# A two-layer Perceiver on one core: the two 1024 x 1024 layers of the last feed-forward as seven quadrant products, and another order of the cross-attention step

## The reference

```python
x = x + L0_xattn(layernorm(x), ctx)      # 16 heads, causal mask
x = x + L0_attn(layernorm(x))            # offsets, gate
x = x + L0_ffn(layernorm(x))             # quantised, 256-768-256
x = x + L1_xattn(layernorm(x), ctx)      # softmax over all 257 keys, no mask
x = x + L1_attn(layernorm(x))            # bias from Pluecker lines
x = x + L1_ffn(layernorm(x))
# L1_ffn, weights ternary, a scale s per output feature:
h = silu((x @ w1.T) * s1) * ((x @ w2.T) * s2)      # 256 -> 1024
h = gelu((h @ h1.T) * s_h1)                        # 1024 -> 1024
h = gelu((h @ h2.T) * s_h2)                        # 1024 -> 1024
return (h @ w3.T) * s3                             # 1024 -> 256
```

## Time and profile before

| what | us |
|---|---|
| median of 3 runs (lowest, highest) | 1780.78 (1777.43, 1781.12) |
| profiled execution, its own time | 1774.97 |
| its span | 1773.2 |
| PE busy, share of the span | 1539.7, 87% |
| DVE, ACT, POOL busy | 823.6, 567.8, 489.8 |
| L765, the two square layers, PE busy, 1024 records | 440.6 |
| L1014, a gelu of 128 x 512 on ACT, mean of one | 0.688 |
| L1547, `c_shift` on POOL, mean of one | 1.042 |
| a 257 KB context's DMA, median from issue to landing (page, part 6) | 2.6 |
| mean granted clock of PE in the profiled execution | 0.965 of full speed |

### The profile page before, as it was taken

How to read it: one execution, slowest core, us unless ns; L and a number is a source line. 1 busy time by engine, 2 the same in 40 slices (tenths; PEclk the granted TensorE clock), 3 DMA queues, 4 the chain that set the end, 5 groups by cost and what they waited for, 6 DMA issues and landing times.

```text
span 1773.2 us, 30285 instructions
## 1 busy us (share of the span) xinstructions
PE 1539.7 (87%) x11788; PEld 978.6 (55%) x11788; DVE 823.6 (46%) x1636; ACT 567.8 (32%) x1409; POOL 489.8 (28%) x581
## 2 busy tenths in 40 slices
PE   4887777891899999999985777699999999999999
PEld 3766665440777777777763555444454454445445
DVE  3889998568645655555554777620011002001000
ACT  2444333577434445444540222220111111101110
POOL 2444332001024545454444888600000000000000
PEclk9999999996899999999996999999999999999999
DMA  7000000000012221111100000020000000000000
GB/s 260 20 9 2 1 0 1 1 0 24 14 48 84 65 83 42 36 42 36 41 13 1 1 1 0 17 103 0 0 12 0 0 0 12 0 0 12 0 0 12
DMA packets 18198, 43.99 MB, mean 25 GB/s; under 512 B 3040, under 2 KB 5600, under 8 KB 16992
## 3 DMA queue, kind: packets, MB, share of 16 engines
q1 hardware_dynamic: 18144, 43.24, 7.4%
HBM read 41.14 MB, written 2.10 MB: 24 GB/s over the span
## 4 chain that ended last, share of the span: by engine, by line
PE 70%; DVE 16%; issue 5%; POOL 4%; ACT 4%; DVEq 1%; DMA 0%; SPq 0%; POOLq 0%; ACTq 0%
PE ps L765 25%; PE ps L411 12%; PE ps L604 6%; PE ps L610 6%; PE ps L417 4%; PE ps L630 4%; PE ps L780 3%; PE ps L582 2%; PE ps L641 2%; POOL lrn L1595 1%; DVE amax L1231 1%; DVE R L1054 1%; DVE nmx L1101 1%; DVE R L1092 1%; DVE R L1169 1%
## 5 line engine op out<-in xcount | busy, mean ns | idle before, releaser
L765 PE MATMUL ps<-R 128*128 128x512 f32 x1024 | 440.6, 592 | 0.0
L765 PEld LDWEIGHTS ps<-R 128*128 128x128 f32 x1024 | 194.3, 190 | 243.5 <-issue 243.5
L411 PE MATMUL ps<-R 128*128 128x128 f32 (+1 forms) x1344 | 308.2, 389 | 7.8 <-DVE R L1227 3.5
L411 PEld LDWEIGHTS ps<-R 128*128 128x128 f32 x1344 | 192.0, 196 | 122.8 <-issue 114.3
L1465 DVE TENSOR_TENSOR R<-ps,w3s 128x256 f32<-128x256 f32 x16 | 6.8, 425 | 465.1 <-PE ps L780 465.1
L1555 POOL TENSOR_TENSOR R<-R,c_inv 128x1024 f32<-128x1024 f32 x64 | 122.4, 1912 | 243.7 <-DVE c_inv L1389 243.7
L963 ACT ACTIVATE R<-ps,c_nmx 128x257 f32<-128x257 f32 x256 | 118.3, 474 | 104.7 <-DVE c_nmx L1378 104.7
L1354 DVE COPY R<-ps 128x512 f32<-128x512 f32 x128 | 88.5, 692 | 128.5 <-PE ps L630 128.5
L610 PE MATMUL ps<-x_wv,R 128*128 128x256 f32 x512 | 132.1, 382 | 0.0
L604 PE MATMUL ps<-R,x_wk 128*128 128x256 f32 x512 | 125.3, 387 | 2.3 <-DVE R L1365 1.2
L604 PEld LDWEIGHTS ps<-R,x_wk 128*128 128x128 f32 x512 | 94.4, 192 | 21.5 <-issue 9.2
(11 more groups left out here) (178 smaller groups left out, 2297.6 us busy)
## 6 DMA issues: line engine op xcount, KB each, us to landing
R<-in_ctxT SPq DMA_DIRECT2D x64, 257.0 KB, 2.6
R<-in_f_h SPq DMA_DIRECT2D x4, 1024.0 KB, 5.1
R<-in_f_h SPq DMA_DIRECT2D x1, 4096.0 KB, 12.6
R<-in_f_w SPq DMA_DIRECT2D x3, 1024.0 KB, 5.4
R<-in_ctxk SPq DMA_DIRECT2D x16, 128.0 KB, 2.3
out<-x SPq DMA_DIRECT2D x4, 512.0 KB, 2.6
x<-in_x SPq DMA_DIRECT2D x1, 1792.0 KB, 8.3
R<-in_a_wqkv SPq DMA_DIRECT2D x1, 768.0 KB, 8.5
```

The costliest lines, as they stand in the source:

```text
L411: r = mm(dst, w[:, ki, fo * P:(fo + 1) * P], src[:, ki, :], start=(ki == 0), stop=(ki == KI - 1))
L765: r = mm(ps[:, ring[o % 4], :], w[:, k, o * P:(o + 1) * P], src[:, k, :], start=(k == 0), stop=(k == NF1 - 1))
```

## The change

1. **Square layers.** `g_block` is replaced by straight code. The activations `f_a`, `f_b` of a block of 512 tokens are held as quadrants: features in two halves of 512, tokens in two halves of 256 (`B11`, `B12`, `B21`, `B22`), with four sums of them (`T1` to `T4`; `T3` overwrites `B12`). The weights are four 512 x 512 quadrants, three of which are used as they are (`A11`, `A12`, `A22`), and four sums (`S1` to `S4`). A layer is four groups `f`; in each, seven products of 4 matmuls with 256 columns go to halves of four PSUM banks (groups take banks 0 to 3 and 4 to 7 in turn). `g_open` makes the product of `A11` and `B11`, `g_close` the other six. ACT copies the first product to SBUF; seven additions on DVE make the partial sums and the four quadrants of the result (`g_close` of DVE, all 128 x 256); ACT applies four gelus of 128 x 256. In the first square layer DVE then makes the four `T` sums of the next layer (`g_sums`), and in `g_first` those of the first one. `g_turn(b+1)` now stands behind the two `g_open` that begin the second layer, and `g_norm(b+1)` on DVE behind the group f = 0 of the first.
2. **Weights.** They no longer lie in SBUF. During the cross-attention SP loads the quadrants of one layer (4 x 1 MB), POOL makes the four sums in 8 additions of 128 x 1024, one per step in steps 8 to 15 and 28 to 35, and SP stores them to a DRAM tensor. At n = 44 SP loads `w1`, `w2`, `w3` and the weights of the first two groups. `load_weights(g)` brings 7 x 128 x 512 values (1.835 MB) in two DMAs, with rows of 2 KB, into a ring of three places, once group g-3 is done: 32 such loads.
3. **Block edges.** `g_first` takes all eight banks, and its first output waits for fewer additions of the block before; `w3` takes four banks.
4. **Cross-attention.** `c_outputs` and `c_extract` are those of sequence n-2 and stand right behind the scores and the maxima; `c_keys` comes ahead of the wait for `c_otc`, and both halves of the values stand together between the two transposes. POOL's loop is written out; the others stay loops.

PE in the cross-attention, the step u = 1, before: L620 scores, L417 projection, L604 keys, L630 transposes, L610 values, L641 outputs.

The diff, cut to SP's loads, the steps of PE and DVE and the sums of POOL:

```diff
+            def load_quadrants(m):
+                for k, q in enumerate((0, 1, 3, 2)):
+                    sp.dma_start(c_quad[k], A["f_hq"][m, q].rearrange("p f c -> p (f c)")).then_inc(quad_in, 16)
+            def store_sums(m):
+                sp.wait_ge(quad_sum, 8 * (m + 1))
+                for k, q in enumerate((4, 5, 2, 1)):
+                    sp.dma_start(sums[m, k].rearrange("p f c -> p (f c)"), c_quad[q]).then_inc(quad_out, 16)
+            def load_weights(g):
+                m, f, r = g // 4 % 2, g % 4, g % 3
+                after(sp, g_prod, product_no(g - 3, 3))
+                sp.dma_start(f_wr[r][:, 0:3, :], A["f_hq"][m, 0:3, :, f, :].rearrange("q p c -> p q c"))\
+                    .then_inc(g_wr[r], 16)
+                sp.dma_start(f_wr[r][:, 3:7, :], sums[m, :, :, f, :].rearrange("q p c -> p q c"))\
+                    .then_inc(g_wr[r], 16)
             for i in range(T - 1):
                 for u in range(SPT):
                     n = SPT * i + u
                     sp.wait_ge(v_ready, n + 1)
                     sp.dma_start(c_ctx[u], A["ctxT"][n + SPT]).then_inc(ctx_in[u], 16)
-                if i < len(later):
-                    sp.wait_ge(f0_x, 1 + T)
-                    sp.dma_start(later[i][0], later[i][1]).then_inc(in_w["ffn"], 16)
+                    if n == 3:
+                        sp.wait_ge(f0_x, 1 + T)
+                        load_quadrants(0)
+                    if n == 18:
+                        store_sums(0)
+                    if n == 22:
+                        sp.wait_ge(quad_out, 64)
+                        load_quadrants(1)
+                    if n == 38:
+                        store_sums(1)
+                    if n == 44:
+                        sp.wait_ge(quad_out, 128)
...
                 c_scores(u)
+                if not (first and u < 2):
+                    if u == 2 and not first:
+                        pe.wait_ge(c_x, i)
+                    if u == 3 and not last:
+                        pe.wait_ge(s["xnT_copied"], N1 + i + 2)
+                    c_outputs(n - 2, (u + 2) % SPT)
+                more = not (last and u >= 2)
+                behind = not (first and u == 0)
+                if more:
+                    pe.wait_ge(ctx_shifted, n + 3)
+                    pe.wait_ge(k_copied, n + 2)
+                    c_keys((u + 2) % SPT)
                 after(pe, c_otc, n - 1)
...
                     c_query(i + 1)
-                more = not (last and u >= 2)
-                behind = not (first and u == 0)
-                if more:
-                    pe.wait_ge(ctx_shifted, n + 3)
-                    pe.wait_ge(k_copied, n + 2)
-                    c_keys((u + 2) % SPT)
                 if behind:
                     pe.wait_ge(c_nrm, n)
                     c_turn_probs(n - 1, (u + 1) % 2, 0)
                 if more:
                     pe.wait_ge(v_copied, n + 2)
-                    c_values((u + 2) % SPT, 0)
+                    for c in range(2):
+                        c_values((u + 2) % SPT, c)
                 if behind:
                     c_turn_probs(n - 1, (u + 1) % 2, 1)
-                if more:
-                    c_values((u + 2) % SPT, 1)
-                if behind:
-                    if u == 1 and not first:
-                        pe.wait_ge(c_x, i)
-                    if u == 2 and not last:
-                        pe.wait_ge(s["xnT_copied"], N1 + i + 2)
-                    if u == 3 and not last:
-                        pe.wait_ge(n_q2, i + 2)
...
+                    project(ps[:, 2 * (o % 4), :], f_w1, f_xnT, o)
+                    project(ps[:, 2 * (o % 4) + 1, :], f_w2, f_xnT, o).then_inc(g_ab, 1)
+            def product(g, w, src, k, bk, half):
+                for ki in range(4):
+                    r = mm(ps[:, 4 * (g % 2) + bk, half * HALF:(half + 1) * HALF], f_wr[g % 3][:, w, ki * P:(ki + 1) * P],
+                           src[:, k, ki, :], start=(ki == 0), stop=(ki == 3))
+                return r
+            def g_open(b, h, f):
+                g = 8 * b + 4 * h + f
+                src = f_b if h else f_a
+                pe.wait_ge(g_wr[g % 3], 32 * (g // 3 + 1))
+                if h == 0:
+                    pe.wait_ge(g_h, NF1 * b + (5, 7, 7, 7)[f])
+                else:
+                    pe.wait_ge(g_c, quadrant_no(8 * b + 3, 11))
+                if h or f >= 2:
+                    pe.wait_ge(g_sum, sum_no(g - 2, 11))
+                product(g, A11, src, B11, 0, 0).then_inc(g_p1, 1)
+            def g_close(b, h, f):
+                g = 8 * b + 4 * h + f
+                src = f_b if h else f_a
+                done = 8 * b + 4 * h + 4
+                used = h or f >= 2
+                if h:
+                    pe.wait_ge(g_c, quadrant_no(8 * b + 3, 12))
+                if h and f == 1:
+                    pe.wait_ge(g_xTc, min(2 * b + 4, 2 * NB))
+                pe.wait_ge(g_T2, done)
+                if used:
+                    pe.wait_ge(g_sum, sum_no(g - 2, 21))
+                product(g, S2, src, T2, 1, 0).then_inc(g_prod, 1)
+                pe.wait_ge(g_T3, done)
+                if used:
+                    pe.wait_ge(g_sum, sum_no(g - 2, 12))
+                product(g, S3, src, T3, 2, 0).then_inc(g_prod, 1)
+                pe.wait_ge(g_T1, done)
+                if used:
+                    pe.wait_ge(g_u, partial_no(g - 2, 4))
+                product(g, S1, src, T1, 3, 0).then_inc(g_prod, 1)
+                pe.wait_ge(g_p1c, g + 1)
+                product(g, A12, src, B21, 0, 1).then_inc(g_prod, 1)
+                pe.wait_ge(g_T4, done)
+                pe.wait_ge(g_u, partial_no(g, 2))
+                product(g, A22, src, T4, 1, 1).then_inc(g_prod, 1)
+                pe.wait_ge(g_u, partial_no(g, 3))
...
+                if not (first and u < 2):
+                    c_extract(n - 2, (u + 2) % SPT)
                 if u == 1 and not first:
...
-                    c_extract(n - 1, (u + 3) % 4)
...
+            def g_close(b, h, f):
+                g = 8 * b + 4 * h + f
+                bk = [[ps[:, 4 * (g % 2) + i, k * HALF:(k + 1) * HALF] for k in range(2)] for i in range(4)]
+                p1, u2 = f_p1[:, g % 2, :], f_u2[:, g % 2, :]
+                dve.wait_ge(g_prod, product_no(g, 6))
+                dve.wait_ge(g_p1c, g + 1)
+                v.tensor_tensor(u2, bk[1][0], p1, ALU.add).then_inc(g_u, 1)
+                dve.wait_ge(g_prod, product_no(g, 7))
+                dve.wait_ge(g_u, partial_no(g, 2))
+                v.tensor_tensor(f_u3, bk[2][0], u2, ALU.add).then_inc(g_u, 1)
+                dve.wait_ge(g_prod, product_no(g, 5))
+                dve.wait_ge(g_u, partial_no(g, 3))
+                after(dve, g_c, quadrant_no(g - 1, 22))
+                v.tensor_tensor(f_c22, bk[3][0], f_u3, ALU.add).then_inc(g_sum, 1)
+                v.tensor_tensor(f_u4, bk[3][0], u2, ALU.add).then_inc(g_u, 1)
+                dve.wait_ge(g_prod, product_no(g, 2))
+                after(dve, g_c, quadrant_no(g - 1, 11))
+                v.tensor_tensor(f_c11, bk[0][1], p1, ALU.add).then_inc(g_sum, 1)
+                dve.wait_ge(g_prod, product_no(g, 4))
+                after(dve, g_c, quadrant_no(g - 1, 21))
+                v.tensor_tensor(f_c21, bk[1][1], f_u3, ALU.add).then_inc(g_sum, 1)
+                dve.wait_ge(g_prod, product_no(g, 3))
+                dve.wait_ge(g_u, partial_no(g, 4))
+                after(dve, g_c, quadrant_no(g - 1, 12))
+                v.tensor_tensor(f_c12, bk[2][1], f_u4, ALU.add).then_inc(g_sum, 1)
+                if h == 0:
+                    dve.wait_ge(g_c, quadrant_no(g, 11))
+                    dve.wait_ge(g_c, quadrant_no(g, 12))
+                    v.tensor_tensor(f_b[:, T1, f, :], f_b[:, B12, f, :], f_b[:, B11, f, :], ALU.subtract).then_inc(g_T1, 1)
+                    dve.wait_ge(g_c, quadrant_no(g, 22))
+                    dve.wait_ge(g_c, quadrant_no(g, 21))
+                    g_sums(f_b, f, 8 * b + 4 + f + 1)
...
+            def quadrant_sum(m, k):
+                part, half = k // 2, slice(k % 2 * QUAD // 2, (k % 2 + 1) * QUAD // 2)
+                dst, a, b, op = ((4, 2, 3, ALU.add), (5, 4, 0, ALU.subtract), (2, 0, 2, ALU.subtract),
+                                 (1, 1, 5, ALU.subtract))[part]
+                if k == 0:
+                    pool.wait_ge(quad_in, 64 * (m + 1))
+                if part:
+                    pool.wait_ge(quad_sum, 8 * m + k - 1)
+                p.tensor_tensor(c_quad[dst][:, half], c_quad[a][:, half], c_quad[b][:, half], op).then_inc(quad_sum, 1)
```

233 lines of the change are left out of this document (150 added, 83 removed).

## The result

The changed kernel takes 1721.17 us (median of 4 runs, 1717.61 to 1723.3), the kernel before 1780.95 beside it (4 runs, 1777.43 to 1782.12): ratio 0.9666, 95% interval 0.9642 to 0.9689. I had predicted 1722, range 1702 to 1752, faster with 0.91. The profiled execution took 1719.48 us with a span of 1717.7: 55.5 us less than the profiled one of before (1774.97), where my sum said 58.5.

A forecast was written before the change was run, and what follows sets the result against it. PE, busy for 87% of the span, was taken as the bound. Terms -52.2 + 3 + 4.2 - 1.5 + 0 - 12 = -58.5 us on 1774.97 gave 1716.5 profiled, 1722 for the median; range 1702 to 1752.

The forecast's parts named there:

- Square layers, -52.2: Eight square layers: 224 records of 256 columns at 216.1 ns, 48.41 us a layer instead of 54.93, -52.2 us.
- Rival (c): Square layers: records of 256 columns take 258 ns, +75 us, 1797 us, slower; chance 0.06 with the weight-load rule.
- Waits and hand-overs of a product, +3: Square layers: a wait every 8 records, 0.034 us each by w1/w2, over 224 products; 0 to +7.6, taken as +3 us.
- The normalisation, +4.2: First square layer: g_norm(b+1) on DVE delays an addition PE wants in group 1; 1.4 us in three blocks, +4.2 us.
- Edges, -1.5: Block edges: the 0.50 us from the end of w3 to the next w1 goes at three edges, -1.5 us.
- the stream, 0: Weight loads of 1.835 MB per group: 6.6 us a load with at least 13.8 us given, costed at 0.
- rival (b): The weights' stream binds: 18.2 us a load, a block of eight 145 us against 139, +24 us, 1746 us; chance 0.08.
- The order, -12: Cross-attention order: steps of 7.3, 6.3, 6.7 and 5.9 us, -1.0 to -0.8 a round, 15 rounds, -12 us.
- my two new waits: Cross-attention: PE's projection waits 0.7 us in u = 1 behind c_stat, and 0.3 us in u = 2 behind c_scale.
- What I had named as the sign: Cross-attention: a round at 26.2 us, with PE's longest wait at the projection in u = 1, would show the forecast right.
- rival (a): Cross-attention: the order gives nothing or costs, margins about 0.0 us; 1734 us, or 1752 at 0.3 more per step; chance 0.14.
- Rival (d): Cross-attention: the gates for POOL's multiplication and c_extract open early, 1706 us; chance 0.10.

The follow-up runs named there:

- Experiment 4: The changed kernel with the product of S2 and T2 made twice in each group, eight products instead of seven: 1770.04 us, ratio 0.9928 to the kernel before.
- experiment 3: The changed kernel with g_norm(b+1) on DVE behind group f = 1 instead of f = 0: 1713.46 us, ratio 0.9615 to the kernel before.
- experiment 5: The changed kernel with 0.79 MB more loaded behind each of 29 of the 32 weight loads, read by nothing: 1717.98 us, ratio 0.9638 to the kernel before.
- experiments 1 and 2: 1: changed kernel with the old cross-attention order, 1731.67 us, ratio 0.9722. 2: kernel before with only the new PE and DVE order, 1768.9 us, ratio 0.9929.
- experiment 9: The changed kernel with the keys split in two halves around the outputs in every step (split keys): 1717.91 us, ratio 0.9672 to the kernel before.

## Why the prediction was right

**Square layers, -52.2.** Right. The last block's two layers take 96.69 us against 109.87 before, -13.18 a block, -52.7 in all. Experiment 4 shows that it is seven products for eight, less 2.6 us for the narrower records. Rival (c), 258 ns a record, is out.

A row first: 448 loads of 190 ns lie beside 448 matmuls in 96.69 us. The Trainium skill, "TensorE: Matmul & The Clock Gate", Part 3, The mechanism, has a load overlap matmuls in flight only for another row group. The trace disagrees, here as with `w3`. The Trainium skill, "TensorE: Matmul & The Clock Gate", Part 2, Step-by-step, lets the load also go ahead when it targets a background weight buffer. The trace agrees in so far as the loads do go ahead; no run here shows the buffer itself.

**Waits and hand-overs of a product, +3.** Wrong, it is 0: 448 records with 56 products' waits show none. I had taken the price from the 27.73 us of `w1` and `w2`, as if their 0.26 us above 64 x 429.2 ns lay between the records. They lie at the start, where PE had stood still at the block's edge. The weight loads of before show it:

```profile
1312.14 0.30 PEld L411 LDWEIGHTS ps<-R 128*128 128x128 f32 x2 [0.92 <-DVE R L1465]
1312.67 0.19 PEld L411 LDWEIGHTS ps<-R 128*128 128x128 f32 x1 [0.24 <-issue]
```

From 1312.67 on they come every 0.43 us. Without the wait at the edge the 64 records take 27.47 us.

**The normalisation, +4.2.** Right in size and place: 1.4 us in each of three blocks, for the addition named, and experiment 3 gives back 4.2. Inside it two errors cancel: the addition was done 7.9 us behind group 0 (1204.21 against 1196.30) instead of 8.3, and PE stood for 1.15 us; the other 0.25 us lie in the restart (144 records take 31.32 us where 144 x 215.8 ns are 31.08).

**Edges, -1.5, and the stream, 0.** The edges gave the 0.50 to 0.60 us counted at each of the three, -1.6, and beside it the 0.26 us above in three blocks, -0.8. The stream is right, and rival (b) is out: no wait of PE for a DMA behind 1150 us, and experiment 5 adds 43% of bytes for nothing. A load is there 7.3 us behind its first issue (the second DMA, issued 0.41 us later, takes 6.9), where 13.8 were free; my 6.6 us from the rate of the contexts was 0.7 short. The loads at n = 44 are 6.7 MB, some 24 us by that rate and not 22.

**The order, -12.** The size was right (10.3 in the pair of profiles, about 12 and 11.9 in experiments 1 and 2, 0.86 us a round), its working only half. Steps were 7.07, 6.18, 6.92 and 6.10 against 7.3, 6.3, 6.7 and 5.9. One term is missing: the outputs read what DVE's second copy writes. It ends 1.33 us behind the start of the second transposes (DVE's copy of 538.20 lasts 0.69 us); transposes and scores are through at some 1.15. PE goes on at 1.39 (538.95), so by the starts each step loses 0.24 us; the list of waits has 0.17 of it, 9.5 us over 58 steps. Against that my two new waits were too large: the one of the projection in u = 1 was 0.16 instead of 0.7, as PE itself came later and the maxima began at 2.01 (539.57) instead of 2.12; the one of u = 2 was not there. The errors cancel, and that the size came out is luck in that part. What I had named as the sign, PE's longest wait at the projection, was therefore wrong: the sum of waits stands at the outputs. The margins of 0.0 us of rival (a) held, since PE came 0.24 us later than I had it. Rival (d), gates that open early, did not come either: a round takes 26.25 us, not 1 us less than the forecast's 26.2.

**What the sum had not.** +4.5 us in stretches without an edit, and the first `w1`, which takes 30.69 us instead of 29.50. Busy time by stretches of 5 us (PE, PEld, DVE, ACT, POOL, granted clock, DMA share, GB/s), after:

```profile
1150.00:1155.00 5.00, 4.31 (x10) 2.21 (x9) 0.00 (x0) 2.48 (x3) 0.00 (x0) 0.50 0.11 36
1155.00:1160.00 5.00, 5.00 (x10) 1.97 (x9) 0.77 (x2) 0.69 (x1) 0.00 (x0) 0.72 0.00 0
```

and before:

```profile
1155.00:1160.00 5.00, 4.13 (x11) 2.47 (x11) 0.00 (x0) 2.48 (x3) 0.00 (x0) 0.50 1.08 465
1160.00:1165.00 5.00, 5.00 (x11) 2.07 (x10) 0.75 (x1) 0.69 (x1) 0.00 (x0) 0.88 0.54 226
```

PE has stood nearly idle for the normalisation in both, and the clock is 0.50 (1.2 GHz) at the first `w1`. A mean of 0.72 over 1155 to 1160 means 2.8 of those 5 us at half speed, so up to 1157.8, 6.0 us from the start of `w1`; before, 0.88 gives 1.2 us, up to 1161.2, 3.6 us from its start at 1157.56. The 2.4 us more at half speed are the 1.2 us. Why it rose later is open: PE has the same instructions ahead of it. It is no price of the change either. The first `w1` takes 29.50 to 30.71 us over the fourteen profiled executions, and 29.62 in experiment 9, whose feed-forward is that of the kernel after.

In all: -52.7 for the layers, +4.2, -1.6, -0.8 at the start of `w1` and +1.2 in the first of them are the feed-forward's -49.8 to 0.1; with -10.3, +2.9 and +1.6 that is -55.6, against 55.5 measured. My sum was 3.3 us short of the gain in the feed-forward, 1.7 too large in the cross-attention, and had 0 for the 4.5 of the other stretches. That the median came within 1 us of 1722 is luck in part: the two medians lie 59.8 us apart, the two profiled executions 55.5, and my sum was 58.5.

## What to carry to other kernels

When seven block products with extra additions replace eight (Strassen's scheme), count a product at the pitch of the narrowest matmul that is already dense in the same trace, and put the extra additions against the gap to the next product of PE: here one product in eight came off nearly whole (2.6 us of 55.3 went to the narrower records), and the only wait was an unrelated block of work standing in the same queue, to be moved one group on. When work is put ahead in an engine's order, list every operand that it reads and when that is written, not only the operands of what used to wait. If two gates close within a few tenths of a microsecond, taking one away gives nothing, as in the step u = 1 of the split keys. Compare stretches instead of whole runs where the parts without an edit wander by 3 us, and the rounds of a loop where there is one: they repeat here within 0.02 us and tell a gain of 0.07 us a round.
